# Seven of the seventeen message tiles of an attention round, made by GpSimd instead of VectorE

## The reference, cut to what matters

```python
h = relu(layernorm(x))
q, k = h @ Wq + bq, h @ Wk + bk                  # v = k
scores = einsum('edh,edh->eh', q[src], k[dst])
attn = softmax of scores over the edges of one src
x = x + segment_sum(attn * k[dst], src) @ Wo + bo
h = relu(layernorm(x))
agg = segment_sum(h[src], dst) / max(in_degree, 1)
x = x + h @ W1.T + b1 + agg @ W2.T + b2
```

## Time and profile before

| what | us |
|---|---|
| median of 3 runs | 2423.22 (2420.7 to 2424.81) |
| the profiled execution: its own time | 2420.92 |
| its span in the trace | 2419.2 |
| busy in the span: PE, DVE, ACT, POOL | 1796.8, 1529.1, 796.9, 883.3 |
| POOL's busy time that is the attention's gather, 425 instructions | 407.8 |

### The profile page before, as it was taken

How to read it: one execution, slowest core, us unless ns; L and a number is a source line. 1 busy time by engine, 2 the same in 40 slices (tenths; PEclk the granted TensorE clock), 3 DMA queues, 4 the chain that set the end, 5 groups by cost and what they waited for, 6 DMA issues and landing times.

```text
span 2419.2 us, 28089 instructions
## 1 busy us (share of the span) xinstructions
PE 1796.8 (74%) x5635; PEld 1017.9 (42%) x5635; DVE 1529.1 (63%) x2795; ACT 796.9 (33%) x2924; POOL 883.3 (37%) x897
## 2 busy tenths in 40 slices
PE   0488840787777777777777877836559999999998
PEld 0243320455455555555555555512224444444443
DVE  8999978776786776776776776514444343434341
ACT  5111102364655655654655655512210000000000
POOL 2000002442342342432432432000047777777771
PEclk9999965788788788788788788879989999999999
DMA  4022223543443443443443443023357777766772
GB/s 135 31 75 65 65 66 105 153 139 118 119 148 110 124 146 107 125 144 108 125 147 105 129 140 108 9 75 114 114 170 205 220 201 209 209 204 193 217 205 82
DMA packets 129612, 318.17 MB, mean 132 GB/s; under 512 B 38126, under 2 KB 38376, under 8 KB 129446
## 3 DMA queue, kind: packets, MB, share of 16 engines
q0 software_dynamic: 70240, 229.93, 32.5%
q1 hardware_dynamic: 59206, 86.80, 11.4%
HBM read 280.81 MB, written 35.86 MB: 131 GB/s over the span
## 4 chain that ended last, share of the span: by engine, by line
DVE 30%; PE 29%; issue 20%; DMA 14%; DVEq 2%; SPq 2%; POOL 1%; ACT 0%; another core or an unknown queue 0%; PEld 0%; POOLq 0%; PEldq 0%; ACTq 0%
PE sums L683 8%; PE wide L638 7%; PE sums L770 7%; DMA nodes<-x 6%; PE wide L709 5%; DVE nodes L1198 4%; DMA node<-h2tab 4%; DVE arena L909 4%; DVE arena L908 3%; DVE nodes L1143 3%; DMA out<-node 3%; DVE nodes L1188 2%; POOL arena L436 1%; DVE node L1086 1%; DVE q_win L1004 1%
## 5 line engine op out<-in xcount | busy, mean ns | idle before, releaser
L436 POOL DMA_INDIRECT arena<-ktab,idx x425 | 407.8, 960 | 705.3 <-DVEq L1193 554.1
L683 PE MATMUL sums<-nodes,oh 128*125 128x260 f32 x1768 | 534.0, 453 | 88.3 <-DVE nodes L1143 88.3
L638 PE MATMUL wide<-w_sb,node 128*125 128x512 f32 x1000 | 479.4, 629 | 38.7 <-DVEq L1020 33.8
L436 POOL DMA_INDIRECT arena<-h2tab,idx x425 | 447.2, 1052 | 153.2 <-issue 132.9
L512 ACT ACTIVATE nodes<-arena,nodes 128x64 f32<-128x64 f32 x2040 | 489.3, 332 | 0.0
L683 PEld LDWEIGHTS sums<-nodes,oh 128*125 128x125 f32 x1768 | 387.2, 224 | 184.9 <-DVE nodes L1143 99.6
L709 PE MATMUL wide<-q_win,node 125*128 125x512 bf16 x1275 | 366.8, 432 | 39.7 <-DVEq L1197 26.4
L770 PE MATMUL sums<-arena,oh 128*125 128x512 f32 x850 | 375.1, 599 | 8.5 <-DMA arena<-h2tab,idx 8.4
L1188 DVE TENSOR_TENSOR nodes<-wide,arena 128x1024 f32<-128x1024 f32 (+1 forms) x225 | 258.4, 1157 | 97.1 <-PE wide L709 97.1
L638 PEld LDWEIGHTS wide<-w_sb,node 128*125 128x125 f32 x1000 | 193.7, 200 | 271.0 <-issue 256.8
L709 PEld LDWEIGHTS wide<-q_win,node 125*128 125x128 bf16 x1275 | 181.0, 145 | 187.0 <-issue 73.9
(11 more groups left out here) (185 smaller groups left out, 1293.7 us busy)
## 6 DMA issues: line engine op xcount, KB each, us to landing
node<-node_tab SPq DMA_DIRECT2D x27, 531.2 KB
q_win<-qtab SPq DMA_DIRECT2D x26, 375.0 KB
qtab<-q_win SPq DMA_DIRECT2D x25, 375.0 KB
arena<-ktab,idx POOLq DMA_INDIRECT x425, 3.8
arena<-h2tab,idx POOLq DMA_INDIRECT x425, 4.4
node<-h2tab SPq DMA_DIRECT2D x26, 250.0 KB
nodes<-x SPq DMA_DIRECT2D x1, 6250.0 KB
ktab<-node SPq DMA_DIRECT2D x25, 250.0 KB
```

Of the source, the lines that this page charges most:

```text
L436: gp.indirect_dma_start(rows[:, b, t, :], None, tab, bass.IndirectOffsetOnAxis(ap=idx[:, b, t:t + 1], axis=0)).then_inc(s["rows_in"][b][PA ...
L638: last = pe.matmul(out, ncol[:, b, c, :], w_sb[:, w, c, :], start=start and c == 0, stop=stop and c == KC - 1)
L683: last = pe.matmul(halves[:, u, :], oh[:, 1 - b, t, :], sums_in[:, t, u, :], start=t == 0, stop=t == CT - 1)
```

## The change

The four multiplications of a round that make message tiles 0 to 6 leave VectorE's program and stand in GpSimd's, at the head of its round, ahead of the gather. GpSimd waits for `exp_ready` for them, signals `msg_ready` as VectorE did, waits for its own messages and frees parts 0 and 1 of `rows`. The wait and the frees at n == 1 leave VectorE's program. The shapes, the groups and the last round stay as they are.

```diff
@@ gpsimd
             gather(at, ktab, 0, 0)
 
+            def messages(g, b):
+
+                gp.wait_ge(exp_ready, g + 1)
+                for t0, k in M_GROUPS:
+                    for u in range(2):
+                        weights = ex[:, u * HH:(u + 1) * HH, t0:t0 + k].rearrange("p h t -> p t h").unsqueeze(3).to_broadcast([128, k, HH, DH])
+                        out, k_rows = (v.rearrange("p t (h d) -> p t h d", h=HH) for v in (msgs[:, t0:t0 + k, u, :], rows[:, 1 - b, t0:t0 + k, u * HD:(u + 1) * HD]))
+                        last = gp.tensor_tensor(out, k_rows, weights, ALU.mult)
+                    last.then_inc(msg_ready, 1)
+                hold(gp, "pool", msg_ready, (g + 1) * len(M_GROUPS))
+                for part in range(2):
+                    gp.sem_inc(at["rows_free"][part], 1)
+
             def attend(g, b, i):
+                messages(g, b)
                 with gp.If(g + 1 < count):
                     gather(at, ktab, g + 1, 1 - b)
             chunks(gp, count, attend)
@@ vector, attend
                 decode(at, g + 1, 1 - b, i + b, 5, 4)
-                messages(g, b, M_GROUPS, msg_ready)
 
                 made, summed = [], []
@@ vector, attend, in the loop over n
-                    if n == 1:
-                        dve.wait_ge(msg_ready, g * len(M_GROUPS) + len(M_GROUPS))
-                        for part in range(2):
-                            dve.sem_inc(at["rows_free"][part], 1)
                     if n > 0:
```

## The result

The changed kernel takes 2442.41 us (median of 4 runs, 2441.3 to 2447.65), the kernel before 2423.49 beside it (4 runs, 2420.7 to 2424.81): a ratio of 1.0091, 95% interval 1.0058 to 1.0125. It is slower by 18.9 us, and the forecast of 2435 missed by 7. Where the executions of one kernel fall into a faster and a slower group, a ratio here is that of the faster group. The profiled execution's span is 2439.6 us against 2419.2, 20.4 more; its mean granted clock is 0.856 against 0.860.

A forecast was written before the change was run, and what follows sets the result against it. VectorE's start of its first product was taken to set each round; 12 x 0.6 + 13 x 0.5 = 13.7 us on the profiled 2420.92 gives 2435, with 2374 to 2490 for 8 in 10.

The forecast's parts named there:

- The sign and the reason: Whole kernel: slower, chance 0.61, because GpSimd's running multiplications hold VectorE's scalar operations and casts; forecast 2435 us.
- The first product: VectorE's first product of a `wide` group, taken to set the round; forecast 0.6 or 0.5 us later in each round.
- the first kind: The 12 rounds whose first VectorE operation waited for nothing new; +0.6 us each. In the 13 others it came late.
- M3: Third of GpSimd's four multiplications in a round, forecast from 922.82 to 924.52 in the round shown.
- M4: Fourth of GpSimd's four multiplications in a round, forecast to end at 926.9 in the round shown.
- The other covers: Gather 1.9 us later behind 13 us of cover, TensorE's tile 0 not deciding, VectorE's third-group wait unchanged: no cost.
- The clock adds nothing that I count: TensorE runs at the 1.2 GHz level after its idle time in both kernels, so the clock was counted as nothing.
- Not held up: Rival, chance 0.18: GpSimd's multiplications don't hold VectorE's small operations; GpSimd then decides, 47 us faster, 2374.
- The multiplications are short: Rival, chance 0.09: GpSimd's multiplications take under 1.9 us, held or not; 2356 to 2416 us.
- It comes out even: Rival, chance 0.12: GpSimd's multiplications take about 2.0 us each; 2416 to 2426, not told from no change.
- Held up more: Rival, chance 0.19: multiplications of 2.6 us or more, or line 1161 or the product waits too; 2470, three passes 2499.
- Port kept: Rival, chance 0.06: GpSimd doesn't give the port back between its four multiplications; +3.6 us in 25 rounds, 2511.

## Why the forecast was right, point by point

**The sign and the reason** were right: small operations of VectorE are held by GpSimd's running multiplication, and the 4 us that VectorE gives away come back as standing still. Putting the multiplications behind the decode ends the hold (0.17 to 0.78 us a line), and a delay with GpSimd untouched gives the same time.

**The first product** was forecast 0.6 later in the first kind and 0.5 counted in the other, 13.7 us in all. Measured as the mean of 24 rounds in the two traces, it starts 7.85 us after `exp_ready` instead of 7.27, +0.58, and 24 x 0.58 = 13.9. That agreement is partly luck. By kind it isn't there: in the first kind the product starts 0.97 later (6.87 to 7.84), where I had 0.6; in the other it starts 0.18 later on the mean of 12 rounds (7.68 to 7.86), near the 0.2 and 0.3 of the two rounds that I worked out, and I took 0.5. And two errors cancel in it:
- *The length of a multiplication* was taken as 2.2 and 1.7 us, and is 1.93 and 1.49. They also start 0.08 us after the exponential instead of 0.2, and without gaps. M3 is over some 5.3 us after the exponential (M4 starts at 938.95), where my working had 6.5.
- *Line 1086* (now 1100) was let through: "Line 1086 ends 0.70 later". It is held like the other three, 2.09 us instead of 0.78. In the timeline above line 1098 ends at 939.01, and 1100 would have been over at 939.71 and the product started 0.44 behind, 6.5 us after `exp_ready`, where it started 6.87 after in the kernel before. So with the measured lengths and no hold of line 1086, my working would have forecast a small gain.

The step behind the second error was "gets in ahead of the next", read from GpSimd's memset, which had let two operations pass. At the end of M3 one waiting operation gets in, GpSimd's next one starts at the same moment, and VectorE's next is held again; at the end of M2 two got in. The sentence "a scalar operation or cast of VectorE stands still until GpSimd's running instruction ends" was too wide as well: lines 1094 and 1096 weren't held, and the trace of before has a cast of one element beside the second memset of rows 7:

```profile
12.85 0.15 DVE L821 CAST lane<-bit_i 128x1 f32<-128x1 int32 x1
```

The product, with one input in PSUM, wasn't held, as I had it.

The Trainium skill ("SBUF — State Buffer", Who interferes with whom) has this hold for scalar operations in the two-port modes and, against a GpSimd instruction that reads SBUF, for operations with two SBUF inputs; an operation with one SBUF input outside those modes is free of it. The traces agree on all three: 1.80 us for 8 elements, 5.17 for 1.82, and 2.36 for the pair of products beside 6.73 us of multiplications. What sets lines 1093, 1094 and 1096 apart from the held ones, no run here shows.

The Trainium skill ("GPSIMD Engine Reference", Performance versus the Vector engine) has 2.2 ns for an element of such an operation. Here it is 1934 / 1024 = 1.9 ns, and the measurement decides.

**The other covers** held. VectorE's wait at the third group is 0.86 us, unchanged. The gather starts 8.1 us after `exp_ready`, 0.3 later than before (925.86 - 918.04 = 7.8) and not 1.9, since the multiplications are shorter, and its last issue ends 29.1 us after it (962.72; I had about 31), with nobody waiting. In this round TensorE's tile 0 could start at 937.57, 4.0 us after the exponential's end, and didn't decide.

**What failed** is one sentence: "The clock adds nothing that I count." A round grew by 1.14 us, not by the 0.58 of its first product. In each trace I added up the time in which the granted clock is at the 1.2 GHz level, round by round. It is 17.07 us in some rounds and 20.48 in the others: 20 and 4 in the kernel before, 12 and 12 in the changed kernel and in both kernels with a memset. The mean is 17.64 us in the kernel before and 18.77 in the other three, and the mean round less that mean is 27.3 us in all four (taken round by round, the difference is 26.5 to 28.1). Windows view of two rounds in a row of the kernel before, the first with the longer low stretch and the second with the shorter:

```profile
962.28:1009.65 47.37, 35.85 (x130) 24.23 (x129) 33.74 (x58) 25.53 (x104) 16.14 (x17) 0.78 0.41 120
1009.65:1054.30 44.65, 34.53 (x130) 23.34 (x129) 32.41 (x53) 25.53 (x103) 16.13 (x17) 0.81 0.42 128
```

The rounds with the longer low stretch are the long ones. The kernel before has 20 of 24 rounds at 44.2 to 44.8 us (44.5 on the mean) and 4 at 47.1 to 47.4. The changed kernel has 12 at 45.1 to 45.2 and 12 at 47.0 to 47.1, though its first product starts at 7.83 to 7.87 in all of them. So most of the cost is not a shift of each round: eight more long rounds are 8 x 2.5 = 20 us, and the twelve that stayed short grew by 0.65 us each, 8 us; the four that were long already are 0.2 us shorter. So the 24 rounds cost 27.3 us where I had 13.7. The second layer's 9.1 us less then brought the whole back near the forecast, by luck. That layer takes 583.9, 576.7, 584.8, 588.6, 582.6, 582.7 and 580.0 us in the seven other kernels on such chips, without order by edit, so I count its 9.1 us as scatter of the execution. Why it varies, and what makes the low stretch longer in one round and not in the next, isn't settled.

**The rivals.** *Not held up* fell: the four lines that I named are held. *The multiplications are short* came near with its length (under 1.9, and it is 1.93) and had the wrong sign, because of the fourth hold. *It comes out even* had the nearest length, about 2.0, and fell for the same reason: the interval of the ratio, 1.0058 to 1.0125, leaves out 1. *Held up more* has a part of the truth, a hold further down the line than I had. *Port kept* fell: an operation gets in after each of the first three multiplications.

## What to carry to other kernels

- Work moved from VectorE to GpSimd is gone from VectorE only if GpSimd does it while VectorE runs operations that it doesn't hold. Here four scalar operations stood still until GpSimd's instructions ended, and 4.0 us saved came back as 4.6; multiplications with both inputs in SBUF were held as well (5.17 us for 1.82).
- Then look at who reads the result. Placed behind the small operations, with the sums of the slower messages two groups later in TensorE's program, the same move gives 0.9675 instead of 1.0091 (the later sums alone were tried only on a chip of the first sort, where they lose 0.8%).
- A delay on the path can cost more than itself: 0.6 to 0.8 us made 1.1 us a round here, with TensorE's time at its low clock growing by as much on the mean.

## What the runs showed of the hardware that I had not expected

- Between two back-to-back instructions of GpSimd a waiting small operation of VectorE passes, and GpSimd isn't delayed by one as small as these: M3 takes 1.50 us, as it does in the kernel with the multiplications behind the decode. (The cast of 800 elements in rows 7 ran into a memset that took 2.32 us, where the other memset's rate gives 1.79.) How many pass differs: two at the end of M2 (lines 1091 and 1093), one at the end of M3, behind which the next is held for a whole further multiplication (1.17, then 2.09 us). The operations of one element weren't held at all (0.14 and 0.20 us). It is the same in all 24 rounds.
- Two engines that both multiply from SBUF take turns: 5.17 us for 1.82, and 4.53 for 3.83.
- GpSimd starts 0.08 us after ScalarE's release (933.62 to 933.70), faster than the 0.24 that VectorE takes between dependent operations of its own.
- One kernel took 2418.8 to 2423.5 us on some chips and 2821 to 2831 on others. On the latter, the first sort, the traces have waits of VectorE's product for something that they call remote (171.8 to 318.0 us in all), which those of the second sort don't have. Waits view of the kernel before with later sums, on such a chip:

```profile
DVE nodes L1188 <- remote: 203.3, 30, 12.7
DVE nodes L1188 <- issue: 87.9, 39, 11.4
```

The changed kernel's ratio is the same on both sorts (1.0091 and 1.0093), but that of the multiplications behind the decode is 0.9946 on the second sort and 1.0242 on the first. What differs between the chips wasn't found, and a small gain should be measured on more than one of them.
